# Every fourth head of the latent attention bounded and weighed on GpSimd

## The reference, cut to what matters

```python
c_kv = x_kv @ W_kv_down.T
c_sel = c_kv[jnp.arange(b)[:, None, None], indices]
kv = (c_sel @ W_kv_up.T).reshape(b, nq, K, 2, H, HD)
scores = jnp.einsum('bqhd,bqkhd->bqkh', q, k) * SCALE
attn = jax.nn.softmax(scores, axis=2)
out = jnp.einsum('bqkh,bqkhd->bqhd', attn, v).reshape(b, nq, d)
```

## Time and profile before

| what | value |
|---|---|
| time, median of 3 runs | 3829.47 us (3828.81 to 3829.94) |
| the profiled execution, its time | 3828.33 us |
| its span in the trace | 3826.5 us |
| mean granted TensorE clock | 0.932 of full speed |
| DVE L1571, the weighing | 256 instructions, 168.5 us |
| POOL's own work | 740 instructions |

### The profile page before, as it was taken

The page is one execution under the profiler, slowest core; times in us unless marked ns, Lnnn a source line. Parts: engine busy times, 40 slices in busy tenths (PEclk is TensorE's granted clock), DMA queues, the critical chain, the costliest instruction groups (busy, mean ns, idle before and its releaser), DMA issues.

```text
span 3826.5 us, 58993 instructions
## 1 busy us (share of the span) xinstructions
PE 3238.3 (85%) x22354; PEld 2244.7 (59%) x22402; DVE 2824.9 (74%) x4915; ACT 2083.5 (54%) x4816; POOL 923.2 (24%) x740
## 2 busy tenths in 40 slices
PE   2568989898898989889898998989889888988877
PEld 2245656666565666656556665656656566665655
DVE  4687786868778687777868778786877868687622
ACT  2356555565665556556564655656566565655432
POOL 1423050221404122150411305031230503124000
PEclk8679999999999999999999999999999999999988
DMA  5212041412304132140413215041320504132110
GB/s 185 81 60 93 24 142 48 144 70 80 134 15 149 51 135 79 54 157 17 149 51 127 87 41 170 17 145 56 123 91 31 168 29 139 61 114 94 47 42 17
DMA packets 205692, 336.50 MB, mean 88 GB/s; under 512 B 23968, under 2 KB 175008, under 8 KB 190688
## 3 DMA queue, kind: packets, MB, share of 16 engines
q1 hardware_dynamic: 205408, 332.72, 25.5%
HBM read 311.66 MB, written 20.97 MB: 87 GB/s over the span
## 4 chain that ended last, share of the span: by engine, by line
PE 60%; DVE 21%; ACT 13%; issue 5%; DMA 1%; SPq 0%; POOL 0%; DVEq 0%; ACTq 0%
PE ps L627 7%; PE ps L608 5%; PE ps L860 4%; PE ps L940 4%; DVE nm L1558 3%; PE ps L639 3%; PE ps L794 3%; PE ps L780 3%; PE ps L770 3%; PE ps L879 3%; PE ps L825 3%; PE ps L745 3%; PE ps L806 2%; PE ps L552 2%; PE ps L839 2%
## 5 line engine op out<-in xcount | busy, mean ns | idle before, releaser
L1322 POOL TENSOR_TENSOR region_x<-region_x 128x512 f32<-128x512 f32 x512 | 645.6, 1273 | 340.3 <-DVE region_x L1535 340.0
L1535 DVE TENSOR_TENSOR_SCAN region_x<-ps,region_x 128x512 f32<-128x512 f32 x512 | 614.8, 1214 | 68.6 <-ACT ps L1061 65.6
L1061 ACT ACTIVATE ps<-region_x,aneg 128x255 f32<-128x255 f32 x1024 | 441.7, 473 | 348.2 <-DVE region_x L1535 341.4
L1302 POOL TENSOR_TENSOR region_x<-region_x 128x512 f32<-128x512 f32 x96 | 122.5, 1276 | 1209.8 <-ACT region_x L1009 1204.8
L1314 POOL TENSOR_TENSOR region_x<-region_x 128x512 f32<-128x512 f32 x128 | 162.5, 1270 | 1030.7 <-DVE region_x L1515 894.2
L1558 DVE TENSOR_REDUCE nm<-ps 128x4 f32<-128x1024 f32 x256 | 308.8, 1222 | 65.8 <-PE ps L608 57.6
L879 PE MATMUL ps<-xTy,wide 128*128 128x256 f32 x1280 | 310.7, 391 | 1.5 <-DVE region_y L1722 1.3
L1210 ACT ACTIVATE region_y<-ps,rmax 128x256 f32<-128x256 f32 x512 | 236.0, 495 | 116.7 <-DVE rmax L1663 116.7
L1515 DVE TENSOR_TENSOR region_x<-region_x,ps 128x512 f32<-128x512 f32 x384 | 254.6, 667 | 20.5 <-PE ps L552 20.3
L879 PEld LDWEIGHTS ps<-xTy,wide 128*128 128x128 f32 x1280 | 237.6, 192 | 41.1 <-issue 8.7
L1571 DVE SCALAR_TENSOR_TENSOR region_x<-region_x,cntk 128x512 f32<-128x512 f32 x256 | 168.5, 690 | 114.6 <-ACT region_x L1102 114.6
(11 more groups left out here) (249 smaller groups left out, 6913.3 us busy)
## 6 DMA issues: line engine op xcount, KB each, us to landing
region_x<-rows_of_dt SPq DMA_DIRECT2D x1024, 128.0 KB, 2.9
wide<-in_wgate SPq DMA_DIRECT2D x16, 1280.0 KB, 7.2
wide<-in_wup SPq DMA_DIRECT2D x16, 1280.0 KB, 10.1
down<-in_wmoe SPq DMA_DIRECT2D x16, 1280.0 KB, 5.5
wide<-in_wq SPq DMA_DIRECT2D x16, 1024.0 KB, 7.0
wide<-in_wk SPq DMA_DIRECT2D x16, 1024.0 KB, 8.8
wide<-in_wv SPq DMA_DIRECT2D x16, 1024.0 KB, 10.6
down<-in_wo SPq DMA_DIRECT2D x16, 1024.0 KB, 13.2
```

The lines of the kernel that those rows point to most:

```text
L1061: last = f(ps[:, 1 + 2 * (k % 2), half * T + 1:(half + 1) * T], dt_rep[k % SLOTS][:, 1:T], ACT.Exp, scale=aneg[:, k, half:half + 1])
L1322: nc.gpsimd.tensor_tensor(hbuf[k % HSLOTS], hbuf[k % HSLOTS], csb, ALU.mult).then_inc(hc_ready, 1)
L1535: nc.vector.tensor_tensor_scan(flat(hbuf[k % HSLOTS]), ps[:, 1 + 2 * (k % 2), :], flat(hbuf[k % HSLOTS]), 0.0, ALU.mult, ALU.add).then_inc ...
```

## The change

Heads n = 1, 5, 9 and 13, the second of each group, are taken from DVE and given to GpSimd. There the bound and the product are two instructions, with a wait for the first between them. GpSimd does them behind the Mamba work of the sequence and ahead of the convolution sums of the next. PE waits for two semaphores where it waited for one. DVE's pieces keep their places: the four empty ones still yield.

```diff
+        pool_bounded, pool_weighed = sem("pool_bounded"), sem("pool_weighed")
...
-                ready = a.weighed if a.masked else a.probs
...
                 def times_v(t):
-                    pe.wait_ge(ready, at(i, 16, 4 * t + 4))
+                    if a.masked:
+                        pe.wait_ge(a.weighed, at(i, 12, 3 * t + 3))
+                        pe.wait_ge(pool_weighed, at(i, 4, t + 1))
+                    else:
+                        pe.wait_ge(a.probs, at(i, 16, 4 * t + 4))
...
+                pool.wait_ge(cntk_sb, i + 1)
+                for t in range(4):
+                    pool.wait_ge(att0.probs, at(i, 16, 4 * t + 2))
+                    p = att0.PT[:, (4 * t + 1) % 8]
+                    nc.gpsimd.tensor_scalar(p, p, 4.0, None, ALU.min).then_inc(pool_bounded, 1)
+                    pool.wait_ge(pool_bounded, at(i, 4, t + 1))
+                    nc.gpsimd.tensor_tensor(p, p, cntk[:], ALU.mult).then_inc(pool_weighed, 1)
                 if i + 1 < B:
                     conv_sums(i + 1)
...
                     for n in range(16):
                         yield
+                        if n % 4 == 1:
+                            continue
                         v.wait_ge(a.probs, at(i, 16, n + 1))
```

## The result

| | before | after |
|---|---|---|
| median of 20 runs each | 3827.14 us | 3833.56 us |
| ratio | | 1.0019, 95% interval 1.0012 to 1.0025 |
| the profiled execution, its span | 3826.5 us | 3832.2 us |

The changed kernel is slower by 6.4 us, 0.19%: inside my range, inside what I called no change, and clear of zero with 20 runs a side. (The 3829.47 us that the prediction was built on was the median of the first three of these runs; the median of the 20 lies 2.3 us lower.)

The account below looks back on a forecast made before the run. PE's queue was taken to bound the kernel, with DVE's weighing 0.63 us early. Terms: 0 for 15 sequences, +1.0 us for sequence 0, 0 for PE's wait; from the 3829.47 us median to 3830.4 us, range 3827.5 to 3841.

Parts of the forecast that it names:

- the 1.27 us bound: GpSimd's minimum at 1.27 us, not 0.9: last weighing 0.35 us late in 15 sequences, 5 us; range reached 3836.
- B: Handing over between DVE and GpSimd: 0.25 us per change makes the last weighing late, 9 us, 3839 us; chance 0.07.
- C: PE's added wait before each product with the values: 0.06 us x 64, 4 us, 3834 us; chance 0.06.
- D: First use of a new GpSimd instruction: at most 3.8 us once, in sequence 0, 3834 us; chance 0.05.
- What bounds the kernel: PE's queue alone leads into the last L639; the last weighing has 0.63 us margin; relieving DVE gains 0.
- Rival E: DVE's relief pays: PE's waits for the weighing L1571 vanish, some 8 us faster, 3822 us; chance 0.03.
- The wait in sequence 0: PE waits for head 15, which ends later: +1.0 us once (+0.5 to +1.7 by the minimum's time).
- The minimum: GpSimd's one-input bound on each moved head: estimated 0.9 us, between 0.42 and 1.27.
- rival A: GpSimd's minimum is dear before the last product: decides from 1.1 us; 35 us at 1.6, 92 at 2.54; chance 0.10.
- The product: GpSimd's two-input multiply on each moved head: 1.27 us, as L1302; bf16 counts not priced.
- Holding: DVE and GpSimd instructions sharing SBUF reads laid one behind another; last weighing still 0.4 us early in sequences 1 to 15.
- My signs: Trace after: last L1571 0.4 us before its L639; PE waiting for GpSimd in each sequence would prove it wrong.

## Why the prediction was right, point by point

The range held the time, and in part by luck. The sum behind it, +1.0 us, is too small by 5.4 us. What filled the range up to 3841 was the 1.27 us bound and rivals B, C and D, and none of them is what came: the loss that was measured was in no term. Two terms of the sum were wrong in ways that cancelled.

- *What bounds the kernel* was read rightly: PE's queue leads into L639, and the relief of DVE was worth nothing, in any experiment. Rival E is out. (Its price was added up too high: 1.0 us and 16 times 0.33 us make 6.3 us, not 8.)
- *The wait in sequence 0*: forecast +1.0 us, measured 1.97 - 1.01 = 0.96 us, three times over (both traces of the changed kernel, and the change in sequence 0 only). The way there was another: GpSimd ended head 13 19.02 us behind the first weighing, where I had 18.3, and only head 15 was held behind it, where I had laid both last heads. The two errors cancelled.
- *The missing term* stands behind it: I costed a longer wait at its length. The clock fell behind it, and 4.6 us more were lost there. This is the step that failed, and it is most of the measured cost: "+1.0 us, once" was +5.6 us. Sequence 0 alone costs what the whole change does. The size couldn't have been read off the wait either: behind 1.32 us and 2.79 us the stretch to sequence 1 took 208.7 and 208.9 us, behind 1.83 to 1.97 us it took 212.2 to 212.5.
- *The minimum*: taken at 0.9 us, with 1.27 as the near bound, on the ground that an instruction with one operand less should be cheaper. It took 1.56 us in the mean, 1.49 at the least. The nearest row was the wrong one, and rival A's threshold, 1.1 us, was passed.
- *The product* was taken at 1.27 us; with the bf16 counts it takes 1.16 us where DVE doesn't delay it.
- *Holding.* Heads of DVE behind the product were held to its end, as the earlier trace rows had shown. But I laid the minimum in the same queue, and it holds DVE for some 0.7 us of its time. That is why rival A didn't come: a minimum of 1.56 us left 0.12 us of margin where my reckoning would have had head 15 over 1 us late. The Trainium skill ("SBUF — State Buffer", "SBUF: two separate sides") has the first of the two keep the pair for the whole instruction; for the product the trace agrees (head 14 ends 0.55 us behind its end), for the minimum, by the profile's spans, it doesn't. GpSimd held by DVE, which no row had shown, is seen too: the product takes 1.57 us behind a head of DVE that started 0.14 us earlier, against 1.16 alone.
- *Rival A's price.* With the minimum doubled it came at +78 us for 3.26 us of minimum; I had said 92 us for 2.54.
- *Rivals B and D* didn't come. A head of DVE ends 0.55 us behind GpSimd's product, no more than it takes in a row of several, so the handing over cost nothing; and no minimum, the first included, took over 1.60 us.
- *The third wait* (rival C): 0 forecast, +0.3 us measured, with an interval from -3 to +4.
- *My signs*: I named "PE waiting for GpSimd in each sequence" as what would prove me wrong; it didn't happen. The last weighing was to end 0.4 us ahead; it was 0.12 us.

What stays open: how long the clock stays down behind a longer wait; why sequences 1 to 15, whose last product is never late, cost 5.3 and 5.9 us when sequence 0 is left as before; and whether the halves add up. The cost in sequences 1 to 15 goes with the margin: with 0.12 to 0.17 us left the kernels cost 5.3, 5.9, 4.0 and, in a single run, 2.6 us, with 0.63 us left 0.0 and 0.3. The loss is at the same two places in both traces, and at the one I looked into the clock falls once more. What leads there isn't settled.

## What to carry to other kernels

Moving work off an engine that isn't last anywhere bought nothing here, and three quarters of it cost nothing measurable either; the last group before a dependent chain is where an offload is paid for, so leave that one on the faster engine. An added wait of PE shouldn't be costed at its length alone: look at what runs behind it, and at the granted clock there, and take a range, since here the loss behind it didn't grow with the wait. And before laying two engines' instructions in one queue, find out for each kind of instruction whether it holds the other; the one-input and the two-input kind differed here.

## What the runs showed of the hardware that I had not expected

- GpSimd's `tensor_scalar` on 128x512 f32 takes 1.49 to 1.60 us in the changed kernel (up to 2.03 beside all sixteen heads of DVE), more than its `tensor_tensor` with two inputs (1.27 us with two f32, 1.16 us with f32 and bf16). The Trainium skill ("GPSIMD Engine Reference", "Engine selection") calls one-input work there roughly line-rate; here it is 3.5 times DVE's 0.42 us.
- DVE with two SBUF inputs is held by a one-input GpSimd instruction for its first 0.6 to 0.7 us of 1.56, by a two-input one to its end.
- Behind a wait of 1.01 us PE kept 2.4 GHz in eight traces. Behind a longer one at the same place it fell to 1.2 GHz in all six: for 3.4 us behind 1.32 us and behind 2.79 us, for 13.65 us behind 1.83 and 1.97 us.
